# Routing tables, code visits, first weights and fact copies moved in a two-layer expert and mixer kernel

## What is computed

```python
# expert layer, of normed tokens; 8 experts, at most 320 tokens each (C)
logits = tokens @ gate_weight.T
top1 = jnp.argmax(logits, axis=-1)
mask = jax.nn.one_hot(top1, E)
ranks = jnp.cumsum(mask, axis=0) - 1          # place of a token in its expert's queue
mask = mask * (ranks < C)
dispatch = jnp.einsum('tec,th->ech', sec_mask, tokens)
hmid = gelu(jnp.einsum('ech,ehi->eci', dispatch, wi), approximate=False)
eout = jnp.einsum('eci,eih->ech', hmid, wo)
out = jnp.einsum('tec,ech->th', combine_weights, eout)
# mixer
out = conv3(x) + (cumsum(u * gates) * (v * gates)) @ Wu
# whole
x = x + 0.5 * ffn(layernorm(x)); x = x + mixer(layernorm(x)); x = x + 0.5 * ffn(layernorm(x))
```

## Time and profile before

| | us |
|---|---|
| median of 3 runs | 1138.18 (1138.1 to 1140.88) |
| the profiled execution, its own time | 1136.17 |
| its span | 1134.3 |
| TensorE busy | 1053.2 (93%) |
| VectorE busy | 721.8 (64%) |
| ScalarE busy | 545.7 (48%) |
| GpSimd busy | 147.5 (13%) |

### The profile page before, as it was taken

One profiled execution on the slowest core, in us unless ns is written; L12 is line 12 of the kernel. 1 busy time (PEld: TensorE's weight loads), 2 busy tenths in 40 slices (PEclk: granted clock), 3 DMA queues, 4 the chain that ended last, 5 costly groups with the idle time before them and its releaser, 6 DMA issues.

```text
span 1134.3 us, 20909 instructions
## 1 busy us (share of the span) xinstructions
PE 1053.2 (93%) x7874; PEld 995.7 (88%) x7874; DVE 721.8 (64%) x1088; ACT 545.7 (48%) x853; POOL 147.5 (13%) x135
## 2 busy tenths in 40 slices
PE   8599989999999999399999994999999999999995
PEld 5599989999999999377777774999999999999995
DVE  7356555666576777368776774457767677665652
ACT  5245444555556565155243223355656656544441
POOL 2201111112030210100000012003113031120101
PEclk9599999999999999799999996999999999999998
DMA  8368636475556652400011017445475565654410
GB/s 299 117 223 299 229 118 201 145 255 199 177 198 208 228 180 74 151 21 1 1 38 37 1 68 254 142 149 203 175 246 207 202 213 188 234 197 149 167 39 24
DMA packets 83283, 177.43 MB, mean 156 GB/s; under 512 B 4192, under 2 KB 4704, under 8 KB 83168
## 3 DMA queue, kind: packets, MB, share of 16 engines
q1 hardware_dynamic: 75776, 153.13, 39.6%
q0 software_dynamic: 7168, 23.07, 5.5%
q10 hardware_dynamic: 288, 0.52, 0.1%
HBM read 162.04 MB, written 18.87 MB: 159 GB/s over the span
## 4 chain that ended last, share of the span: by engine, by line
PE 89%; issue 3%; DMA 2%; DVE 2%; ACT 2%; POOL 1%; POOLq 0%; SPq 0%; DVEq 0%; ACTq 0%
PE psH L1183 13%; PE psH L1184 12%; PE psH L1185 12%; PE acc L1191 11%; PE acc L1192 11%; PE acc L1190 11%; PE acc L1183 3%; PE acc L1184 3%; PE acc L1185 3%; PE psT L1235 1%; PE psT L1399 1%; PE psH L1307 1%; PE acc L1355 1%; PE psH L1355 1%; DMA rows<-out_x,src_now 1%
## 5 line engine op out<-in xcount | busy, mean ns | idle before, releaser
L1183 PE MATMUL psH<-dth,wih 128*128 128x240 f32 (+5 forms) x1024 | 297.4, 290 | 15.2 <-issue 14.5
L1184 PE MATMUL psH<-dtl,wih 128*128 128x240 f32 (+5 forms) x1024 | 295.8, 289 | 0.0
L1185 PE MATMUL psH<-dth,wil 128*128 128x240 f32 (+5 forms) x1024 | 295.6, 289 | 0.0
L1191 PE MATMUL acc<-htl,woh 128*128 128x240 f32 (+5 forms) x1024 | 293.3, 286 | 0.0
L1192 PE MATMUL acc<-hth,wol 128*128 128x240 f32 (+5 forms) x1024 | 293.1, 286 | 0.0
L1190 PE MATMUL acc<-hth,woh 128*128 128x240 f32 (+5 forms) x1024 | 293.1, 286 | 0.0
L763 DVE TENSOR_TENSOR wol<-raw_wo,woh 128x1024 fp32r<-128x1024 f32 x128 | 155.7, 1223 | 140.2 <-ACT woh L594 139.3
L1183 PEld LDWEIGHTS psH<-dth,wih 128*128 128x128 f32 x1024 | 195.5, 191 | 19.2 <-issue 18.4
L628 ACT ACTIVATE gel<-psH 128x320 f32<-128x320 f32 x256 | 112.0, 438 | 206.3 <-PE psH L1185 201.5
L1184 PEld LDWEIGHTS psH<-dtl,wih 128*128 128x128 f32 x1024 | 195.4, 191 | 0.0
L1185 PEld LDWEIGHTS psH<-dth,wil 128*128 128x128 f32 x1024 | 195.4, 191 | 0.0
(11 more groups left out here) (188 smaller groups left out, 1144.7 us busy)
## 6 DMA issues: line engine op xcount, KB each, us to landing
raw_wi<-in_wi SPq DMA_DIRECT2D x64, 1024.0 KB
raw_wo<-in_wo SPq DMA_DIRECT2D x64, 1024.0 KB, 5.4
out_x<-xt SPq DMA_DIRECT2D x4, 1024.0 KB, 5.1
xt<-in_x SPq DMA_DIRECT2D x6, 512.0 KB, 8.4
xt<-x SPq DMA_DIRECT2D x3, 1024.0 KB, 9.4
raw_u<-in_wuT SPq DMA_DIRECT2D x1, 1024.0 KB
raw_u<-in_wvT SPq DMA_DIRECT2D x1, 1024.0 KB
xt<-x SPq DMA_DIRECT2D x4, 256.0 KB, 3.2
```

Source lines behind the costliest of these rows:

```text
L1183: pe.matmul(out, lh, rh, start=first, stop=False)
L1184: pe.matmul(out, lh, rl, start=False, stop=False)
L1185: return pe.matmul(out, ll, rh, start=False, stop=last)
L1191: pe.matmul(out, lh, rl, start=False, stop=False, skip_group_check=True)
```

## The change

Four things change. The table's products follow the ranks and counts with no visit between them; in layer 1 the first four tiles' products go ahead of the ranks. The visits go to the first, third and sixth pair in layer 0 (the first is a hint only), one stands ahead of `earlier` in both layers, and three stand behind the table; behind the fifth pair of layer 0 the code is aligned to a block. GpSimd spreads the facts of the whole first part and VectorE only those of the second part's last tiles (4 in layer 0, 2 in layer 1, as before). In layer 1 SyncE's first weight loads go in between the stores, as soon as the mixer is done with their space. And `stage` and the first norm move from the second to the third pair of an expert.

```diff
+HALF_B = (12, 14)
@@ SyncE, layer 1
-                    for g in range(GROUPS - 1):
-                        sp.wait_ge(d_addu, GROUP * (g + 1))
-                        q = slice(g * GROUP, (g + 1) * GROUP)
-                        sp.dma_start(out_tiles[:, q, :], xt[:, q, :]).then_inc(s.kept, 16)
-                    sp.wait_ge(d_addu, TILES)
...
+                    keep(0)
+                    keep(1)
+                    sp.wait_ge(d_conv, DC * GROUPS)
                 for k in range(2):
                     load_wi(s, 0, k, k)
                 for k in range(2):
+                    if n == 1:
+                        sp.wait_ge(p_uv, GROUP * (GROUPS - 1 + k))
                     load_wo(s, 0, k, k)
+                    if n == 1:
+                        keep(2 + k)
@@ GpSimd, spread_facts
-                r = slice(q.start, (q.start + q.stop) // 2)
+                r = slice(q.start, HALF_B[layers.index(s)] if b else q.stop)
@@ ScalarE, expert
-                        if i >= 1 and not last:
-                            norm_rows(e + 1, h + side, 1 - side, i - 1)
+                        if not last:
+                            for k in ((), (), (0, 1), (2,))[i]:
+                                norm_rows(e + 1, h + side, 1 - side, k)
@@ VectorE, spread_facts, tables, layer 0's head, expert, and the mixer's end
-                r = slice((q.start + q.stop) // 2, q.stop)
+                r = slice(HALF_B[layers.index(s)], TILES)
...
-                dve.wait_ge(s.tabled, BATCHES)
+                dve.wait_ge(s.tabled, 1)
...
-                    spread_facts(0, s)
                     place(1, s)
                     lane(2, s)
-                    spread_facts(1, s)
+                    spread_facts(s)
...
-                        if i == 1 and not last:
+                        if i == 2 and not last:
                             stage(e, h, side, sources)
...
                 lane(2, nxt)
-                spread_facts(0, nxt)
@@ TensorE, tabulate
+                def tabulate(first, end, s=s, n=n):
+                    for t in range(first, end):
                         if t % LT == 0:
                             pe.wait_ge(s.lanes_done, t // LT + 1)
+                        if t == 0:
+                            pe.wait_ge(s.facts_pool, 1)
+                        if t == SPLIT[n]:
+                            pe.wait_ge(s.facts_pool, 2)
+                        if t == HALF_B[n]:
+                            pe.wait_ge(s.facts_dve, 1)
@@ TensorE, the head
+                        if p in (0, 2, 5):
+                            peek()
                         if p == 4:
-                            peek()
+                            pe.addr_align(BLOCK, offset=0, max_nops=0)
                     logits(PAIRED - 1)
                     folds(PAIRED - 2)
                     folds(PAIRED - 1)
-                    peek()
+                peek()
                 earlier()
+                if n == 1:
+                    tabulate(0, LT)
                 ranks(1)
                 take_counts()
-                peek()
-                tabulate(0)
-                peek()
-                tabulate(1)
-                peek()
-                peek()
-                if n == 0:
+                tabulate(LT * n, SPLIT[n])
+                tabulate(SPLIT[n], TILES)
+                for _ in range(3):
                     peek()
```

More of the change, by code:

```diff
@@ L354, in _, with keep @@
                 if n == 1:
-                    for g in range(GROUPS - 1):
+                    def keep(g, s=s):
                         sp.wait_ge(d_addu, GROUP * (g + 1))
@@ L359, in _ @@
                         sp.dma_start(out_tiles[:, q, :], xt[:, q, :]).then_inc(s.kept, 16)
-                    sp.wait_ge(d_addu, TILES)
-                    q = slice((GROUPS - 1) * GROUP, TILES)
-                    sp.dma_start(out_tiles[:, q, :], xt[:, q, :]).then_inc(s.kept, 16)
+                    keep(0)
+                    keep(1)
+                    sp.wait_ge(d_conv, DC * GROUPS)
                 for k in range(2):
@@ L866, in lane, with spread_facts @@
                                   ).then_inc(s.lanes_done, 1)
-            def spread_facts(b, s):
-                dve.wait_ge(s.place_done, b + 1)
-                q = tiles_of(layers.index(s), b)
-                r = slice((q.start + q.stop) // 2, q.stop)
+            def spread_facts(s):
+                dve.wait_ge(s.place_done, BATCHES)
+                r = slice(HALF_B[layers.index(s)], TILES)
                 each = [P, r.stop - r.start, FACTS, Q]
@@ L1295, in take_counts @@
                     ins.then_inc(s.rank_done, 1)
-                def tabulate(b, s=s, n=n):
-                    q = tiles_of(n, b)
-                    for t in range(q.start, q.stop):
+                def tabulate(first, end, s=s, n=n):
+                    for t in range(first, end):
                         if t % LT == 0:
                             pe.wait_ge(s.lanes_done, t // LT + 1)
-                        if t == q.start:
-                            pe.wait_ge(s.facts_pool, b + 1)
-                        if t == (q.start + q.stop) // 2:
-                            pe.wait_ge(s.facts_dve, b + 1)
+                        if t == 0:
[4 more added lines that the diff above has]
+                            pe.wait_ge(s.facts_dve, 1)
                         ins = pe.matmul(psH[0][:, 0:Q * FACTS], at_lane[:, t, :],
@@ L1309, in tabulate @@
                                         start=(t == 0), stop=(t == TILES - 1))
-                    ins.then_inc(s.tabled, 1)
+                    if end == TILES:
+                        ins.then_inc(s.tabled, 1)
                 def peek(n=n):
```

## The result

The changed kernel takes 1146.71 us in the median of 5 runs (1140.68 to 1149.06), against 1138.18 before: the ratio is 1.0064, with a 95% interval of 1.0033 to 1.0096. A second set of runs came to 1149.27 us beside 1139.45, ratio 1.0074 (1.0052 to 1.0096). So it is slower by 0.6 to 0.7%, some 8 us. The forecast was 6 us faster, and the range of 1126.0 to 1137.5 us did not hold the time.

What follows compares the result with a forecast made beforehand. TensorE, busy 93% of 1134.3 us, was taken as the bound. Gains of 2.8 + 2.5 + 0.7 = 6.0 us off the 1138.18 us median gave 1132.2 us, with a range of 1126.0 to 1137.5.

Steps and rivals of the forecast that it cites:

- Part 1: Layer 0's head: moved visits, the alignment and GpSimd's spread of all eight tiles end the table earlier, gaining 2.8 us.
- (a): Layer 0's pairs of tiles: two early visits cost 0.5 us each, 1.0 in all (bounds 0 and 1.3).
- (d): Layer 0's ranks and table: the 2.96 us code wait goes, the table ends at 35.4 instead of 38.2, gain 2.8 us.
- C: Rival, layer 0: the first early visit finds no code, TensorE waits 3.2 us more, 1135.4 us; chance 0.13.
- E: Rival: the new order pushes out code of widths experts run, 4.9 us each, 1142.0 us with two; chance 0.06.
- (b): Layer 0: GpSimd's spread of 768 columns takes 1.5 us from 24.0, delaying VectorE's multiply by 1.0 us.
- Part 2: Layer 1's head: four table tiles before the ranks, visits moved, weight loads between stores; table ends at 689.3, gain 2.5 us.
- Part 3: Experts: copies and first norm move to the third pair, ending a late gather's wait; gain 0.7 us, cost zero.
- B: Rival, layer 0's third expert: its code stays loaded, 4.9 us go, 1127.3 us; chance 0.21.

Runs made afterwards that it cites:

- experiment 2: The changed kernel without the alignment behind layer 0's fifth pair, all else kept: 1129.70 us, ratio 0.9921; second set 1131.23 us, 0.9918.
- experiment 5: The changed kernel itself, run and profiled again with nothing altered, beside the kernel before: 1149.27 us, ratio 1.0074.
- experiment 6: The kernel before with only the alignment added, behind the hint at layer 0's fifth pair: 1145.89 us, ratio 1.0058.
- experiment 8: The changed kernel without the alignment and with the copies of the next facts and first norm back in the second pair: 1135.17 us, ratio 0.9937.

## Why the prediction was wrong

**Where it failed.** In Part 1, the step (a) to (d) named the alignment among what is added and gave it no price of its own; in (d) it even counted as a reason for the gain ("the alignment starts a fresh block behind the fifth pair"). It costs 4.3 us where it stands, 1.7 to 4.1 more at the lower clock behind it and, through the shift, 4.7 ahead of the first expert and 2.4 behind the loop; by the runs it is some 17 us in all (experiments 2 and 5). The reason given in (d) was wrong too: the 2.96 us are gone without the alignment. The trace of before could not show the cost, since TensorE never branches among the pairs there; then it should have been bounded by the nearest rows, as the visits were. They were there: 2.04 and 3.81 us of "issue" where a branch needed code.

**C** had the right kind of event and the wrong place: a branch among the pairs that finds no code. It was tied to the first early visit, which cost next to nothing. **E** was right in kind too: one width and not two, at 4.7 us near its price of 4.9, plus the code behind the loop, of which it had not thought. Its 6% was too little: the row of 3.81 says that one block is already gone when it is wanted, and the change touched the order of every load in layer 0. With the measured 4.3 and 4.7 + 2.4 us, the two together would have given 1132.2 + 4.3 + 7.1 = 1143.6, still short of 1146.71.

**What was right.** Without the alignment the forecast is too small: 9 us against 6.0.

(a) Two early visits: the ranks of the first half came 0.93 us later (21.67 against 20.74 before), forecast 1.0. (b) VectorE's multiply met GpSimd's spread of 768 columns and took 0.86 us against 0.22. VectorE, then GpSimd, without the alignment:

```profile
25.54 0.86 DVE L830 TENSOR_TENSOR r<-r,desc 128x64 f32<-128x64 f32 x1
```

```profile
24.46 1.86 POOL L459 TENSOR_TENSOR at_facts<-at_place,facts 128x768 f32<-128x768 f32 x1 [1.16 <-DVE at_place L864]
```

That is 0.64 us, forecast 1.0, and it ends as the spread ends, at 26.3 to 26.4. The spread itself was mis-sized: 1.86 us from 24.46, forecast 1.5 from 24.0. By the Trainium skill (SBUF — State Buffer, Terms) the two engines share a port pair under an exclusive lock. This pair of rows agrees, and only for the operation that reads two operands in SBUF: the three small ones between 24.90 and 25.51, with an operand in PSUM, took 0.21 or 0.22. (d) The table's products took 6.17 us in one run, not 7.4: the granted clock was 0.50 in their first 3.5 us and 0.72 in the rest. The table was read 4.5 us earlier, forecast 2.8. VectorE, before and without the alignment:

```profile
38.25 0.16 DVE L896 TENSOR_SCALAR src_now<-psH 128x3 int32<-128x3 f32 x1 [7.74 <-PE psH L1307]
```

```profile
33.70 0.16 DVE L902 TENSOR_SCALAR src_now<-psH 128x3 int32<-128x3 f32 x1 [2.07 <-PE psH L1312]
```

Part 2: the ranks stood where the forecast had them (684.0 in the time of before, forecast 684.1), the table ended 0.6 us earlier than forecast, 3.1 us gained by the profile and 2.3 by the runs, forecast 2.5. The gather did not wait for SyncE's stores. Part 3: no cost in the third pairs, as forecast; the gain of 0.7 us was that of one late gather, and other executions lost up to 1.6 us in one and had up to two (experiments 6 and 8), so it was too small.

**The rule that was weighed.** Against B and E the prediction set the Trainium skill (Runtime: NRT & Kernel Launch, Instruction fetch mechanics), whose FIFO of 128 KiB left no ground for either. It does not fit here: the third expert's block had been visited ahead of the loop, and 3.7 to 4.3 us of wait stood ahead of that expert in every kernel. In the kernel before, only six packets of 16 KiB were fetched behind the one at that width's hint (29.87 us) and before its use, where eight blocks should have stayed. The same section of the Trainium skill says that a taken branch to a target outside the current window of two pages forces a fetch before execution goes on. That warning spoke against this change and I did not weigh it; the 4.31, 4.73 and 6.62 us under the alignment agree with it.

**Faster than both.** The changed kernel without the line of the alignment: 1129.70 and 1131.23 us, 0.8% under the kernel before.

## What to carry over

A line that only moves code, an alignment or a padding, is an operation like any other: ask how many slots it skips, where it branches to, and what had fetched that place. Where a row shows that one block of code already has to be loaded twice, any change in the order of the branches can move that loss to a dearer place, so give it a price and a chance of its own. And when several edits come together, price them one by one; here one line undid the gain of all the others.

## What the runs showed of the hardware

The instruction queue moves packets of 16 KiB, and they fall where TensorE waits for code. One took 0.9 to 1.3 us in most cases, and up to 2.4, mostly when two went close together. Of the hints given ahead of 20 us, while the DMA queues were loading weights and tokens (DMA share 1.0), the next fetch began 2.6 to 4.9 us later, and once 9.1 us later; behind 22 us it began 0.0 to 2.5 us later. Whether the other transfers cause that, no run shows. The alignment's branch in the changed kernel took 6.05 us, with two fetches of 1.1 us in it, begun at 15.34 and 18.62. Fillers went by at 0.07 us each. A shift of nearly one block in TensorE's head cost 7 us at two places far behind it (ahead of the first expert and behind the loop), more than the 4.3 us of idle time at the branch that made it.
